# Routed rows added onto stored shared rows in DRAM, in the two mixtures of a four-layer kernel

## What is computed

```python
shared = silu(xt @ sg_w.T) * (xt @ su_w.T) @ sd_w.T
probs = sigmoid(xt @ router_w.T + routing_bias)
topk_p, topk_idx = top_k(probs, 2)              # 2 of 8 experts for each token
w = zeros((T, E)).at[arange(T)[:, None], topk_idx].add(topk_p / topk_p.sum(-1, keepdims=True))
h = silu(einsum('th,eih->tei', xt, wg)) * einsum('th,eih->tei', xt, wu)
routed = einsum('te,teh->th', w, einsum('tei,ehi->teh', h, wd))
return shared + routed
```

## Time and profile before

| | |
|---|---|
| time, median of 3 runs (lowest, highest) | 1954.78 us (1952.68, 1955.26) |
| span of the profiled execution | 1949.9 us |
| mixture one: shared 272 to 404, routed 404 to 737, closing 737 to 865 | 132, 333 and 128 us |
| mixture two: shared 1625 to 1724, routed 1724 to 1883, closing 1883 to 1950 | 99, 159 and 67 us |
| busy over the span: PE, DVE, ACT, POOL | 84%, 74%, 56%, 22% |
| moved by DMA | 164.47 MB, mean 84 GB/s |

### The profile page before, as it was taken

How to read it: one execution, slowest core, us unless ns; L and a number is a source line. 1 busy time by engine, 2 the same in 40 slices (tenths; PEclk the granted TensorE clock), 3 DMA queues, 4 the chain that set the end, 5 groups by cost and what they waited for, 6 DMA issues and landing times. The chain is left out here.

```text
span 1949.9 us, 42092 instructions
## 1 busy us (share of the span) xinstructions
PE 1639.8 (84%) x15122; PEld 940.4 (48%) x15122; DVE 1433.8 (74%) x2776; ACT 1093.3 (56%) x2216; POOL 422.2 (22%) x545
## 2 busy tenths in 40 slices
PE   3987569989999993767999999999997857999950
PEld 2775459966666661221222222222223646977730
DVE  5776777744444446869999999999982877756657
ACT  1444535533333333524999999999996454544422
POOL 3000236612122222220000000000000125844432
PEclk9999669999999996876999999999998957999975
DMA  6700025521111114431121121121003203444445
GB/s 249 282 1 6 1 90 165 165 68 58 58 61 61 58 39 147 119 93 48 37 63 45 39 63 45 39 62 37 18 18 127 87 1 95 141 130 126 128 135 168
DMA packets 113091, 164.47 MB, mean 84 GB/s; under 512 B 20278, under 2 KB 89788, under 8 KB 110588
## 3 DMA queue, kind: packets, MB, share of 16 engines
q1 hardware_dynamic: 97372, 117.85, 20.2%
q0 software_dynamic: 15520, 43.93, 6.0%
HBM read 89.07 MB, written 72.37 MB: 83 GB/s over the span
## 5 line engine op out<-in xcount | busy, mean ns | idle before, releaser
L1511 DVE TENSOR_REDUCE sa_row_max<-psum 128x1 f32<-128x1024 f32 x512 | 582.4, 1212 | 12.2 <-PE psum L1393 12.1
L1494 ACT ACTIVATE sa_probs<-psum 128x512 f32<-128x512 f32 x1024 | 549.7, 597 | 37.8 <-PE psum L1444 28.4
L1393 PE MATMUL psum<-v_k_max,v_q_stack 48*128 48x512 f16 x1024 | 301.3, 398 | 24.1 <-DVE sa_row_max L1511 16.2
L1424 PE MATMUL psum<-sa_probs,sa_v_now 128*32 128x256 f32 (+1 forms) x3840 | 321.2, 406 | 0.1
L1444 PE MATMUL psum<-v_q_stack,sa_k_main 49*128 49x512 f16 x1024 | 309.6, 384 | 2.3 <-ACT sa_probs L1494 1.4
L1988 PE MATMUL psum<-m0w_all,m0fx_xt_high 128*128 x568 | 193.5, 382 | 0.7 <-DVE m0fx_xt_low L1920 0.7
L1444 PEld LDWEIGHTS psum<-v_q_stack,sa_k_main 49*128 49x128 f16 x1024 | 64.7, 94 | 222.8 <-ACT sa_probs L1494 208.5
L1424 PEld LDWEIGHTS psum<-sa_probs,sa_v_now 128*32 128x32 f32 x3840 | 75.7, 108 | 189.7 <-issue 99.9
L1934 DVE TENSOR_TENSOR m0fx_ht_low<-psum,m0fx_ht_high 128x512 f16<-128x512 f32 x71 | 49.1, 692 | 134.4 <-ACT m0fx_ht_high L1902 134.4
L1317 POOL TENSOR_SCALAR sa_max_half<-sa_o_sb 128x128 f16<-128x128 f32 x32 | 9.2, 288 | 553.3 <-ACT sa_o_sb L1485 553.3
L1896 ACT ACTIVATE m0fx_gate<-psum 128x512 f32<-128x512 f32 x71 | 42.4, 597 | 152.6 <-PE psum L1988 152.6
(11 more groups left out here) (355 smaller groups left out, 3380.5 us busy)
## 6 DMA issues: line engine op xcount, KB each, us to landing
x_rows<-la_blank SPq DMA_DIRECT2D x18, 1032.0 KB, 8.8
v_q_stack<-q_scratch SPq DMA_DIRECT2D x192, 64.0 KB, 2.4
m0s_all<-x_rows SPq DMA_DIRECT2D x71, 129.0 KB, 2.0
m1fx_x_in<-x_rows SPq DMA_DIRECT2D x71, 129.0 KB, 2.2
m0fs_stage<-in_up SPq DMA_DIRECT2D x16, 512.0 KB
m0g_got<-y_rows SPq DMA_DIRECT2D x32, 256.0 KB, 3.9
o_scratch<-sa_o_sb POOLq DMA_DIRECT2D x32, 256.0 KB, 2.5
wo_o_in<-o_scratch SPq DMA_DIRECT2D x32, 256.0 KB, 3.7
```

The lines of the kernel that those rows point to most:

```text
L1393: nc.tensor.matmul(mx_ps[m % 2][:, half * 512:(half + 1) * 512], q_stack[h][side:side + ROWS, head, qt * P:(qt + 1) * P], k_max[side:side ...
L1424: last = nc.tensor.matmul(o_ps[32 * g:32 * g + 32, cols], v_now[:, kt, kv, :], probs[(GROUPS * step + g) % 16][:, cols], start=(kt == 0), ...
L1494: nc.scalar.activation(probs[at % 16][:, :], st_ps[bank_of(at)][:, :], ACT.Exp, scale=0.25 / (QK_SCALE * QK_SCALE)).then_inc(s["expd"], 1)
L1511: nc.vector.tensor_reduce(row_max[n % 2][:, at % QT, column:column + 1], mx_ps[m % 2][:, :], AX.X, ALU.max).then_inc(s["maxed"], 1)
```

## The change

The shared rows no longer wait in `core.y` to be added to. A class `Sums` is an array in DRAM of 4096 rows, one for each token, and 128 spare rows. In `shared_expert` SP stores the shared rows of each pair of tiles to the first sum, behind the weight load of an odd step. In `routed_experts` the scatter adds (`compute_op=ALU.add`) instead of writing, so that a token's two routed rows go to one and the same row. Two scatters may touch the same row, so each waits until the scatter before it onto the same sum has landed: with one sum in mixture one that is the scatter just before, with two sums in mixture two, which are used in turn, the one before that. POOL also waits for all 16 stores ahead of the first. The second sum of mixture two starts cleared, not from shared rows. The closing stages load sums: in mixture one straight into `core.y`, in mixture two the first sum into `core.y` and the second into a new array `second`, which DVE adds. A group's transfers have a semaphore of their own, and all loads are issued without waiting. Blank slots now point to the spare row of their partition, so one buffer `blank` serves for all, and the clearing transfers are issued one behind the other; they also clear the spare rows and the second sum. The rows of `x_rows` are written tile by tile (1032 B in one piece) instead of eight rows of a partition at a time.

The core of the diff:

```diff
@linear_attention
+                sp.wait_ge(s["numbered"], 1)
                 for q in range(CHUNKS):
-                    sp.wait_ge(s["numbered"], q + 1)
                     for zero_dram in zero_drams:
-                        flat = zero_dram.rearrange("j p d -> (j p) d").rearrange("(p r) d -> p r d", p=P)
-                        sp.dma_start(flat[:, q * BLANK_TILES:(q + 1) * BLANK_TILES, :], blank[q % 2][:, :, :])\
-                            .then_inc(zeros_out[q % 2], 16)
+                        sp.dma_start(zero_dram.rearrange("j p d -> p j d")[:, q * BLANK_TILES:(q + 1) * BLANK_TILES, :],
+                                     blank[:, :, :]).then_inc(zeros_out, 16)
+                for y in sums:
+                    sp.dma_start(y.spare_rows, blank[:, 0, 0:D]).then_inc(zeros_out, 16)
+                for y in cleared_sums:
+                    for q in range(SUM_CHUNKS):
+                        sp.dma_start(y.by_tile[:, q * BLANK_TILES:(q + 1) * BLANK_TILES, :], blank[:, :, 0:D])\
+                            .then_inc(zeros_out, 16)
...
-                for j in range(2):
-                    nc.gpsimd.memset(blank[j][:, :, :], 0.0).then_inc(s["zeroed"], 1)
-                pool.wait_ge(s["zeroed"], 2)
-                for q in range(CHUNKS):
-                    ge(pool, zeros_out[q % 2], q // 2 * 32)
-                    nc.gpsimd.iota(blank[q % 2][:, :, D].bitcast(I32), pattern=[[1, BLANK_TILES]],
-                                   base=2 * B * N + q * BLANK_TILES, channel_multiplier=SLOT_TILES)\
-                        .then_inc(s["numbered"], 1)
+                nc.gpsimd.memset(blank[:, :, :], 0.0).then_inc(s["zeroed"], 1)
+                pool.wait_ge(s["zeroed"], 1)
+                nc.gpsimd.iota(blank[:, :, D].bitcast(I32), pattern=[[0, BLANK_TILES]], base=B * N,
+                               channel_multiplier=1).then_inc(s["numbered"], 1)
...
+class Sums:
+    def __init__(self, nc, name, starts_shared):
+        self.rows = nc.dram_tensor(name, (B * N + P, D), F32, kind="Internal").ap()
+        self.by_tile = self.rows[0:B * N, :].rearrange("(t p) d -> p t d", p=P)
+        self.spare_rows = self.rows[B * N:B * N + P, :]
+        self.starts_shared = starts_shared
@gathered_residual
-                def load(p):
-                    ge(sp, added, p - HELD + 1)
-                    for c in range(2):
-                        sp.dma_start(got[p % HELD][:, c, :, :], by_choice[:, c, 2 * p:2 * p + 2, :])\
-                            .then_inc(came[p % HELD], 16)
+                def load(g):
+                    for p in pairs_of(g):
+                        sp.dma_start(pair(core.y, p), pair(sums[0].by_tile, p)).then_inc(came[g], 16)
+                        if len(sums) > 1:
+                            sp.dma_start(pair(second, p), pair(sums[1].by_tile, p)).then_inc(second_came[g], 16)
...
-                for p in range(HELD):
-                    load(p)
+                for g in range(2):
+                    load(g)
                 if qkv is not None:
                     weights.sync_load(sp)
                     bias.sync_load(sp)
...
+                for g in range(2, NG):
+                    load(g)
                 for g in range(NG + DRAIN):
-                    for p in pairs_of(g):
-                        if p + HELD < BY_DMA:
-                            load(p + HELD)
...
-                def add_first(p):
-                    dve.wait_ge(came[p % HELD], p // HELD * 32 + 32)
-                    nc.vector.tensor_tensor(pair(core.y, p), got[p % HELD][:, 0, :, :], pair(core.y, p), ALU.add)\
-                        .then_inc(first_added, 1)
                 def add_second(p):
-                    dve.wait_ge(first_added, p + 1)
-                    nc.vector.tensor_tensor(pair(core.y, p), got[p % HELD][:, 1, :, :], pair(core.y, p), ALU.add)\
+                    dve.wait_ge(second_came[p // 2], 32)
+                    nc.vector.tensor_tensor(pair(core.y, p), pair(second, p), pair(core.y, p), ALU.add)\
                         .then_inc(added, 1)
...
                     if g < NG:
-                        for p in pairs_of(g):
-                            add_first(p)
-                        for p in pairs_of(g):
-                            add_second(p)
+                        dve.wait_ge(came[g], 32)
+                        if len(sums) > 1:
+                            for p in pairs_of(g):
+                                add_second(p)
@shared_expert
+                def store_y(p):
+                    sp.wait_ge(s["y_done"], 2 * p + 2)
+                    sp.dma_start(y_sum.by_tile[:, 2 * p:2 * p + 2, :], core.y[:, 2 * p:2 * p + 2, :])\
+                        .then_inc(y_out, 16)
...
+                        if i % 2 == 1 and i >= 5:
+                            store_y(i // 2 - 2)
+                for p in range(n // 2 - 2, n // 2):
+                    store_y(p)
@routed_experts
                 nc.clear_and_free_semaphores(ended)
+                pool.wait_ge(y_out, 16 * (T // 2))
                 for i in range(n):
+                    before = i - len(sums)
+                    if before >= 0:
+                        pool.wait_ge(y_stored[before % 2], (before // 2 + 1) * 16)
                     pool.wait_ge(s["y_done"], i + 1)
                     pool.indirect_dma_start(
-                        y_rows, bass.IndirectOffsetOnAxis(ap=x_in[i % ROWS_HELD][:, D:D + 1].bitcast(I32), axis=0),
-                        y_sb[i % 2][:, :], None).then_inc(y_stored[i % 2], 16)
+                        sums[i % len(sums)].rows,
+                        bass.IndirectOffsetOnAxis(ap=x_in[i % ROWS_HELD][:, D:D + 1].bitcast(I32), axis=0),
+                        y_sb[i % 2][:, :], None, compute_op=ALU.add).then_inc(y_stored[i % 2], 16)
@route
-                nc.gpsimd.iota(r.row_of, pattern=[[P, T], [B * N, 2]], base=0, channel_multiplier=1).then_inc(masks, 1)
+                nc.gpsimd.iota(r.row_of, pattern=[[P, T], [0, 2]], base=0, channel_multiplier=1).then_inc(masks, 1)
@build
-        y_rows = nc.dram_tensor("y_rows", (2 * B * N + SLOT_TILES * P, D), F32, kind="Internal").ap()
+        sums0 = [Sums(nc, "y_sum0", True)]
+        sums1 = [Sums(nc, "y_sum1", True), Sums(nc, "y_sum2", False)]
```

More of the change, by code:

```diff
@@ L568, in linear_attention @@
         bias_kv = ph.sb("bias_kv", [P, 2 * D])
-        blank = [ph.sb(f"blank{j}", [P, BLANK_TILES, ROW]) for j in range(2)]
+        blank = ph.sb("blank", [P, BLANK_TILES, ROW])
         turn_ps = [ph.ps() for j in range(2)]
@@ L583, in linear_attention @@
                                     "z_done", "y_done")}
-        zeros_out = [ph.sem(f"zeros_out{j}") for j in range(2)]
+        zeros_out = ph.sem("zeros_out")
         CHUNKS = SLOT_TILES // BLANK_TILES
+        SUM_CHUNKS = T // BLANK_TILES
+        cleared_sums = [y for y in sums if not y.starts_shared]
+        ZEROED = CHUNKS * len(zero_drams) + len(sums) + SUM_CHUNKS * len(cleared_sums)
         def real(i):
@@ L862, in _ @@
                 slots(slot)
-    return [(zeros_out[j], (CHUNKS + 1 - j) // 2 * 32) for j in range(2)]
+    return zeros_out, 16 * ZEROED
+class Sums:
[4 more added lines that the diff above has]
+        self.starts_shared = starts_shared
 class Norm:
@@ L964, in gathered_residual @@
         y_norm = Norm(ph, "y", rstd_y)
-        got = [ph.sb(f"got{j}", [P, 2, 2, D]) for j in range(HELD)]
-        came = [ph.sem(f"came{j}") for j in range(HELD)]
-        first_added, added, scaled, x_ready = (ph.sem(n) for n in ("first_added", "added", "scaled", "x_ready"))
+        second = ph.sb("second", [P, T, D]) if len(sums) > 1 else None
+        came = [ph.sem(f"came{g}") for g in range(NG)]
+        second_came = [ph.sem(f"second_came{g}") for g in range(NG)] if len(sums) > 1 else None
+        added, scaled, x_ready = (ph.sem(n) for n in ("added", "scaled", "x_ready"))
         if qkv is not None:
@@ L1224, in _ @@
                     if g < NG:
-                        dve.wait_ge(added, 2 * g + 2)
+                        if len(sums) > 1:
+                            dve.wait_ge(added, 2 * g + 2)
                         for i in tiles_of(g):
@@ L1686, in _ @@
                 if filled is not None:
-                    for zeros_out, count in filled:
-                        pool.wait_ge(zeros_out, count)
+                    pool.wait_ge(*filled)
                 for i in range(n):
@@ L2329, in _, with mixture @@
                 dve.wait_ge(s["found"], NG // ROUND)
-def mixture(core, nc, name, F, shared, normalise, bias_row, up_r, down_r, x_rows, y_rows, filled):
+def mixture(core, nc, name, F, shared, normalise, bias_row, up_r, down_r, x_rows, sums, filled):
     with Phase(nc, name) as ph:
         r = Routing(ph)
+        y_out = nc.alloc_semaphore(name + "_y_out")
         with Phase(nc, name + "w") as pw:
```

28 lines of the change are left out of this document (13 added, 15 removed).

## The result

The changed kernel takes 1995.01 us (median, 1994.64 to 1995.28) against 1953.73 us for the kernel before in the same runs (1950.82 to 1955.26): a ratio of 1.0211, 95% interval 1.0197 to 1.0225. Slower, as forecast, but by 41 us where 12.5 were forecast, and 1 us above the top of the range.

A forecast was written before the change was run, and what follows sets the result against it. PE was held to fill shared and routed stages, a ring of waits to set closing stages. Gains of 7.9 us against costs of 20.4 made 1954.8 + 12.5 = 1967.3 us; range 1949 to 1994.

The forecast's parts named there:

- The new wait: Mixture two's routed stage: POOL's wait for the scatter two tiles before, held to add nothing to DVE's existing buffer wait.
- L: Time of an adding scatter from POOL's start to the engine that waits for its landing; taken as 3.75 us.
- The length of an add: Routed stages: an adding scatter taken as 3.75 us, 1.0 more than a plain one's 2.75, with bounds 3.19 and 4.75.
- The rule itself: Mixture two's routed stage: 35 pairs each pay what L has over 3.39 us; forecast cost 12.6 us.
- the handoff: Routed stages: time from a result's start to its own scatter's start; the prediction used 0.75 us in mixture two.
- Mixture one, inside: Mixture one's routed stage: each scatter waits for the one before, but a tile's 4.47 us covers L; cost 0.
- The ends: Ends of both routed stages: last scatters delay the closing stage's first load, 5.1 and 2.0 us; cost 7.1 us.
- Closing stages: Both mixtures' closing stages: fewer DVE adds and earlier loads gain 5.9 and 2.0 us; elsewhere DVE only waits longer.
- Stores and clearing: Shared-row stores cost 0.7 us, one last issue in each mixture; clearing 23.6 MB takes 79 us under cover, cost 0.
- Cheap and free add: Rivals on the scatter: L 3.19, 1951.9 us, chance 0.30; or L still 2.75, 1949.7 us, chance 0.14.
- The dear add: Rival: L is 4.75, so mixture one's scatter chain also becomes a bound; 2027 us, chance 0.06.
- DVE as the bound: Rival: closing stages shrink by all the DVE busy time removed, 33 us, giving 1942 us; chance 0.04.

The follow-up runs named there:

- the load-order kernel: Kernel before, with only weights and biases of mixture one's closing stage issued behind four row loads instead of eight: 1954.86 us, ratio 1.0005.

## Why the prediction was wrong, step by step

**The new wait (failed).** "The new wait on POOL is the same wait and adds none." It is the same event, but it is a second wait ahead of the scatter, and the result's wait, which ends last, stands behind it. It put 0.52 us (means, 0.75 to 1.27) into a loop that had no slack left: 35 x 0.52 = 18.2 us of the 27.7 that were missed. That is a share by reckoning; taking the wait away, or putting it second, gave back 12.4 and 13.3 us. The prediction bounded L from both sides, but put the new wait at nothing.

**The length of an add (mis-sized).** 3.75 was taken; the mean is 4.02, the median 3.93, inside the bounds of 3.19 and 4.75. 35 x 0.27 = 9.5 us, the rest of what was missed. The failed part of it is "POOL's 0.96 us should stay": POOL took 0.59 more. And the base of 2.75 was one row, longer than most: a plain scatter lands after 2.4 us in the median and a result starts 0.08 behind a landing, so an add takes some 1.4 us more than a plain one, not 1.0.

**The rule itself (right).** The slack of 4.14 us for two tiles, and 35 times what goes over it: with 4.02 and 1.27 it gives the 40.3 us measured. With the measured median of 3.93 and the handoff left at 0.75 the prediction's formula gives 19.8 us, so 1975, and with 18.2 more 1993. The runs with more buffers and three sums show that the loop through the buffer was the bound: the tile goes from 2.65 to 2.15 and 2.07.

**Mixture one, inside (right).** Scatter to scatter has the median 4.55 in both traces. A scatter stands up to 5.4 us behind the one before it there, and the two buffers cover that.

**The ends (right in kind, too small).** Mixture one 7.2 against 5.1: the first add in single file took 5.24, not 3.75. Two sums take out most of it. Mixture two: the last but two scatter to the first load is 1928.12 - 1918.99 = 9.13 us against 6.29 before, 2.8 more where 2.0 were forecast; 0.47 of the rest is again the handoff.

**Closing stages (right in size, the reasons only in part shown).** Gains of 6.3 and 1.8 against 5.9 and 2.0. In mixture one most groups kept their distance (12.9 us from one to the next, before and after), so taking work off a DVE that waits gave nothing there. In mixture two the sum came out by luck: a group fell from 6.90 to 6.79 us, half of what was forecast for it, and the first add to x came 1.2 us sooner, not 0.6. In mixture one's head, moving the weights forward was held to be part of the gain. With the adds in place the load order is worth nothing; how the gain divides between the adds that are gone and the earlier weights, no run separates. Nine kernels with no adds in mixture one's closing stage took 126.8 to 129.7 us there, two with four a group 133.6 and 134.9, the one with two 131.6.

**Stores and clearing (right).** The stores cost 1.5 us in this trace, inside the bounds. The clearing kept to its sum: its last transfer was issued at 97.0 us, and the DMA engines were busy until about 110, where 31 + 79 had been reckoned and 158.7 would have done. The 2.0 us by which the first shared stage starts later are not the change's: the load-order kernel, which has the code of before up to there, starts it at 273.9, and the changed code with three sums at 271.3. The last 15 us of the linear attention, before (window, us, busy time of the engines, then PEclk, DMA share, GB/s):

```profile
145.00:160.00 15.00, 7.29 (x50) 6.38 (x50) 6.34 (x18) 2.54 (x5) 0.51 (x1) 1.00 0.02 2
```

and after:

```profile
145.00:160.00 15.00, 8.40 (x37) 7.10 (x36) 5.81 (x18) 1.26 (x2) 0.00 (x0) 0.64 0.00 1
```

The granted clock was 1.00 there before and 0.64 after. It does not settle the start by itself: with four buffers it was 0.74 and the stage started at 271.5. What lowered it no run here shows.

**The rivals.** Cheap and free add fall with 3.93. The dear add's place, mixture one as a second bound, was not reached. DVE as the bound falls with the distances in the closing stages, all but unchanged.

## What to carry to other kernels

When a wait is added ahead of an engine's transfer, ask not only whether its event has long come, but in which order it stands to the wait that ends last: on POOL here the late one second cost 0.48 us a time, and first nothing. An adding scatter has to be priced as a chain (result, start, landing, next result), against the time that the buffers leave; four buffers in place of two took out 32 of the 41 us, and a third target with more buffers and the better order nearly all. An engine that is off the critical path gave next to nothing by doing less, except where its work held up a neighbour that was on it.

## What the runs showed of the hardware that had not been expected

An adding scatter of 128 rows takes POOL 1.55 us against 0.96 for a plain one, whether its rows are 1 KB or 512 B. From its start to its landing it takes 3.8 us against 2.4, and 3.3 with half of the bytes (medians of mixture one). Two waits ahead of one such transfer on POOL cost 0.48 us when the second ends last, and nothing measurable when the first does. A POOL instruction on 128 x 4 values took 2.41 us instead of 0.20 beside DVE's adds.
